# A fused attention and routed feed-forward kernel: a new order of VectorE's and GpSimd's step, and gelus, scores and k's remainder read from PSUM

## The reference, cut to what matters

```python
def _mlp(x, W1, b1, W2, b2):
    return gelu(x @ W1 + b1) @ W2 + b2              # [.., 256] -> [.., 256]

n = layernorm(x)
q, k, v = _mlp(n, ..q), _mlp(n, ..k), _mlp(n, ..v)
scores = tril(q @ k.T / sqrt(256 * 512))            # no softmax
out = layernorm(scores @ v) * ln_w + ln_b
x = x + out
tile = argmax(position_table @ sign(tile_sigs).T)   # one of 8 tiles for each position
x = x + layernorm(x) @ W[tile].T + b[tile]
```

## Time and profile before

| | before |
|---|---|
| median of 3 runs | 330.68 us (329.66 to 331.28) |
| the profiled execution | 329.83 us, of it 328.1 us span |
| mean granted TensorE clock | 0.947 of full |
| TensorE matmul busy | 281.4 us, 86% |
| TensorE weight load busy | 252.1 us, 77% |
| VectorE busy | 232.0 us, 71% |
| ScalarE busy | 202.5 us, 62% |
| GpSimd busy | 196.8 us, 60% |

### The profile page before, as it was taken

How to read it: one execution, slowest core, us unless ns; L and a number is a source line. 1 busy time by engine, 2 the same in 40 slices (tenths; PEclk the granted TensorE clock), 3 DMA queues, 4 the chain that set the end, 5 groups by cost and what they waited for, 6 DMA issues and landing times.

```text
span 328.1 us, 5585 instructions
## 1 busy us (share of the span) xinstructions
PE 281.4 (86%) x1828; PEld 252.1 (77%) x1828; DVE 232.0 (71%) x538; ACT 202.5 (62%) x402; POOL 196.8 (60%) x227
## 2 busy tenths in 40 slices
PE   5899999799989998899899999999998969996000
PEld 5778988698779888787878898899887969996000
DVE  3799759778987768865876787679569798885000
ACT  2377576667566884587468856966774469991000
POOL 3533506451664787589638854964793557777772
PEclk9579999999999999999999999999999999999555
DMA  8806940200020012001201040100047414943210
GB/s 213 284 0 212 337 156 1 67 31 0 2 91 8 32 65 98 32 33 34 97 2 47 20 128 16 51 1 2 32 122 193 125 53 137 306 145 112 75 54 2
DMA packets 24656, 28.01 MB, mean 85 GB/s; under 512 B 4722, under 2 KB 22386, under 8 KB 24564
## 3 DMA queue, kind: packets, MB, share of 16 engines
q1 hardware_dynamic: 15764, 13.07, 13.6%
q0 software_dynamic: 3488, 8.99, 7.8%
q10 hardware_dynamic: 5376, 5.59, 5.4%
HBM read 13.99 MB, written 14.56 MB: 87 GB/s over the span
## 4 chain that ended last, share of the span: by engine, by line
PE 63%; DVE 17%; POOL 5%; issue 5%; ACT 5%; DMA 3%; POOLq 0%; SPq 0%; DVEq 0%; ACTq 0%
PE ring L427 35%; PE o_ps L427 9%; PE s_ps L427 6%; POOL out_dram L1477 5%; PE sc_ps L427 4%; DMA w_stage<-w1k 3%; PE w_ps L427 2%; DVE xres L1004 2%; PE ring L440 2%; PE ring L669 2%; PE ring L518 1%; DVE hT L930 1%; DVE state L976 1%; DVE kT L942 1%; DVE v L955 1%
## 5 line engine op out<-in xcount | busy, mean ns | idle before, releaser
L427 PE MATMUL ring<-xnT,w_sp 128*128 128x512 f32 x288 | 75.1, 408 | 3.1 <-DVE xnT L925 1.7
L427 PEld LDWEIGHTS ring<-xnT,w_sp 128*128 128x128 f32 x288 | 54.0, 195 | 15.6 <-issue 2.0
L427 PE MATMUL ring<-hT,w_sp 128*128 128x512 f32 x192 | 47.4, 398 | 4.5 <-DVE qT L936 3.0
L726 ACT ACTIVATE h<-ring,b_cols 128x512 f32<-128x512 f32 x48 | 33.0, 687 | 21.1 <-PE ring L427 20.7
L427 PEld LDWEIGHTS ring<-hT,w_sp 128*128 128x128 f32 x192 | 35.0, 188 | 14.2 <-DVE qT L936 4.1
L1392 POOL DMA_INDIRECT sorted_rows<-xres,slot_i x32 | 33.8, 1057 | 8.6 <-issue 6.1
L1356 POOL TENSOR_TENSOR hT<-h,hT 128x512 fp32r<-128x512 f32 x24 | 31.7, 1331 | 4.5 <-ACT hT L729 4.3
L1362 POOL TENSOR_TENSOR vtok<-v,vtok 128x512 fp32r<-128x512 f32 x14 | 17.7, 1284 | 23.8 <-ACT vtok L749 23.8
L1381 POOL TENSOR_TENSOR xres<-ve,half 128x4 f32<-128x4 f32 (+1 forms) x9 | 8.7, 968 | 37.2 <-DVE ve L1024 37.1
L729 ACT CAST hT<-h 128x512 fp32r<-128x512 f32 x48 | 29.8, 620 | 1.5
L976 DVE TENSOR_TENSOR state<-s_ps,state 128x512 fp32r<-128x512 f32 x27 | 18.6, 688 | 16.5 <-ACT state L768 16.5
(11 more groups left out here) (181 smaller groups left out, 635.8 us busy)
## 6 DMA issues: line engine op xcount, KB each, us to landing
sorted_rows<-blank ACTq DMA_DIRECT2D x1, 5070.0 KB, 20.3
xt<-x SPq DMA_DIRECT2D x8, 512.0 KB, 3.6
slot_rows<-sorted_rows SPq DMA_DIRECT2D x23, 130.0 KB, 4.0
h<-sorted_rows SPq DMA_DIRECT2D x16, 130.0 KB, 2.7
w_stage<-tile_w SPq DMA_DIRECT2D x8, 256.0 KB, 4.0
hT<-position_table POOLq DMA_DIRECT2D x1, 512.0 KB, 7.1
sorted_rows<-xres,slot_i POOLq DMA_INDIRECT x32, 2.7
row_stage<-rows ACTq DMA_DIRECT2D x1, 384.0 KB, 8.1
```

What stands on the lines that cost most here:

```text
L427: last = te.matmul(o, lhs[k][a], rhs[k][c], start=start and k == 0 and i == 0, stop=stop and k == n - 1 and i == 2, skip_group_check=check)
L726: nc.scalar.activation(h32[:, m, :], ring[(2 + m) % 3][:, :], ACT.Gelu, bias=b1c[:, m // 2, m % 2:m % 2 + 1]).then_inc(gelu, 1)
```

## The change

What it does, by engine:

- **ScalarE**: gelu of halves 0, 2, 4 writes back into its own `ring` bank, and the rounding copy reads it there. The lead norm's four chunks are spread: one after half 4, one after q, one between k and v, one between v's halves. The squares of chunks 2 and 3 follow half 5.
- **VectorE**: `h_rest` reads the `ring` bank, `k_rest` reads k's bank and adds the bias itself, the mask writes the scores back into `sc_ps`, and `scores_rest` reads them there (group 7 keeps `sc32`). `h_rest` of half 0 stands at the head of the step, that of 2 ahead of chunk 2's state, that of 4 ahead of chunk 3. `x1_stats` and `x1_var` of group s move from the end of step s to step s + 1, behind `h_rest` of half 0. Negation and epsilon of `lead_var` and `x1_var` go to GpSimd (two small operations each).
- **TensorE**: a bank whose half belongs to VectorE is free when `h_rest` is done, not when gelu is; v's second half and ktok wait for `k_lo` where they waited for `k_full`; the scores wait for `sc_lo` of the group before.
- **GpSimd**: the step is half 1, `residual(s + 1)`, half 3, `rstd_lead`, `rstd_x1`, two scatters, [step 3: `tile_shifted(4)`], half 5, `rstd_out`, two scatters, `v_rest`, `tile_shifted`. Group 0's four scatters move from step 2 to step 1, group 1's stay in step 2.

```diff
+            def bank_free(s, m):
+                if m in DVE_H:
+                    te.wait_ge(h_lo_dve, len(DVE_H) * s + DVE_H.index(m) + 1)
+                else:
+                    te.wait_ge(gelu, 6 * s + m + 1)
...
                     if m >= 3:
-                        te.wait_ge(gelu, 6 * s + m - 2)
+                        bank_free(s, m - 3)
...
                     if j < 3:
-                        te.wait_ge(gelu, 6 * s + 4 + j)
+                        bank_free(s, 3 + j)
...
-                        te.wait_ge(k_full, 2 * s + 1)
+                        te.wait_ge(k_lo, 2 * s + 1)
...
-                        te.wait_ge(k_full, 2 * s + 2)
+                        te.wait_ge(k_lo, 2 * s + 2)
...
             def hidden(s, m):
                 act.wait_ge(fill, FILLS * s + 3 + m)
-                nc.scalar.activation(h32[:, m, :], ring[(2 + m) % 3][:, :], ACT.Gelu,
+                full = ring[(2 + m) % 3][:, :] if m in DVE_H else h32[:, m, :]
+                nc.scalar.activation(full, ring[(2 + m) % 3][:, :], ACT.Gelu,
...
-                nc.vector.tensor_tensor(hT[:, m, 1, :], h32[:, m, :], hT[:, m, 0, :].bitcast(F32),
+                nc.vector.tensor_tensor(hT[:, m, 1, :], ring[(2 + m) % 3][:, :], hT[:, m, 0, :].bitcast(F32),
...
-                nc.vector.tensor_tensor(kT[:, 1, j, :], k32[:, j, :], kT[:, 0, j, :].bitcast(F32),
-                                        ALU.subtract).then_inc(k_lo, 1)
+                nc.vector.scalar_tensor_tensor(out=kT[:, 1, j, :], in0=ring[(10 + j) % 3][:, :],
+                                               scalar=b2c[:, K, j:j + 1], in1=kT[:, 0, j, :].bitcast(F32),
+                                               op0=ALU.add, op1=ALU.subtract).then_inc(k_lo, 1)
...
             def rstd_lead(s):
+                pool.wait_ge(aggr1, s + 1)
+                nc.gpsimd.tensor_scalar(nm1[:, :], mv1[:, :, 0], -1.0, None, ALU.mult)
+                nc.gpsimd.tensor_tensor(ve1[:, :], mv1[:, :, 1], eps[:, :], ALU.add).then_inc(var1, 1)
...
             for s in range(LAST):
...
+                h_rest(s + 1, 1)
+                residual(s + 1)
+                h_rest(s + 1, 3)
+                if s + 2 < STEPS:
+                    rstd_lead(s + 2)
+                if s:
+                    rstd_x1(s - 1)
+                if s > 1:
+                    rows_sorted(s - 1, (0, 1))
+                if s == 3:
+                    tile_shifted(4)
+                h_rest(s + 1, 5)
+                rstd_out(s)
```

More of the change, by code:

```diff
@@ L725, in hidden, with q_rounded @@
                 act.wait_ge(fill, FILLS * s + 3 + m)
-                nc.scalar.activation(h32[:, m, :], ring[(2 + m) % 3][:, :], ACT.Gelu,
+                full = ring[(2 + m) % 3][:, :] if m in DVE_H else h32[:, m, :]
+                nc.scalar.activation(full, ring[(2 + m) % 3][:, :], ACT.Gelu,
                                      bias=b1c[:, m // 2, m % 2:m % 2 + 1]).then_inc(gelu, 1)
                 act.wait_ge(gelu, 6 * s + m + 1)
[L729 to L736, removed]
+                nc.scalar.copy(hT[:, m, 0, :], full).then_inc(h_hi, 1)
+            def q_rounded(s, j):
+                if j == 0:
+                    act.wait_ge(o_ready, CH * s)
+                act.wait_ge(fill, FILLS * s + 9 + j)
+                nc.scalar.activation(qT[:, 0, j, :], ring[(8 + j) % 3][:, :], ACT.Identity,
+                                     bias=b2c[:, Q, j:j + 1]).then_inc(q_hi, 1)
             def k_rounded(s):
@@ L744, in k_rounded, with v_rounded @@
                     nc.scalar.copy(kT[:, 0, j, :], k32[:, j, :]).then_inc(k_hi, 1)
[L746 to L749, removed]
+            def v_rounded(s, j):
+                act.wait_ge(v_sum, 2 * s + 1 + j)
+                nc.scalar.copy(vtok[:, 0, 2 * j:2 * j + 2, :], v32[:, 2 * j:2 * j + 2, :]).then_inc(v_hi, 1)
             def scores_rounded(s):
@@ L1018, in x1_var @@
                 alone(dve, gate_dve)
+                if s:
+                    dve.wait_ge(shift3, s)
                 for c in cs:
@@ L1021, in x1_var @@
                 last.then_inc(aggr3, 1)
[L1022 to L1024 removed]
+                if s == LAST:
+                    dve.wait_ge(aggr3, part)
+                    nc.vector.tensor_scalar(nm3[:, these], mv3[:, these, 0], -1.0, None, ALU.mult)
+                    nc.vector.tensor_scalar(ve3[:, these], mv3[:, these, 1], EPS, None, ALU.add).then_inc(var3, 1)
             def tile_rest(t):
@@ L1227, in _ @@
             for s in range(LAST):
+                h_rest(s + 1, 0)
+                if s:
+                    x1_stats(s - 1, range(CH))
+                    x1_var(s - 1, range(CH))
                 state_rest(s, 1)
@@ L1236, in _ @@
                     lead_var(s + 2)
-                h_rest(s + 1, 0)
+                h_rest(s + 1, 2)
                 state_rest(s, 2)
@@ L1251, in _ @@
                     route_tables()
-                h_rest(s + 1, 2)
+                h_rest(s + 1, 4)
                 out_centred(s, 3)
-                h_rest(s + 1, 4)
                 if s == 3:
@@ L1273, in _ @@
                     scores_rest(s + 1)
+                    x1_final(s, (3,))
                     state_rest(s + 1, 0)
                     out_centred(s + 1, 0)
-                    x1_final(s, (3,))
-                    x1_stats(s, range(CH))
-                    x1_var(s, range(CH))
                 else:
```

90 lines of the change are left out of this document (36 added, 54 removed).

## The result

The changed kernel takes 335.99 us (median of 4 runs, 334.82 to 336.45) where the kernel before takes 330.17 beside it (4 runs): a ratio of 1.0167 [1.0126, 1.0209]. Forecast were 335.7 us, from 331.9 to 339.0.

What follows compares the result with a forecast made beforehand. TensorE was taken to bound the loop, GpSimd's output scatters the end. Terms 1.2 - 1.3 - 0.1 - 1.8 - 0.2 + 4.3 + 2.9 = +5.0 on 329.83 gave 334.8, or 335.7 us on the medians' scale; range 331.9 to 339.0.

Steps and rivals of the forecast that it cites:

- Step 3, the largest term: TensorE stands 6.5 us at tile 4's weights until GpSimd's tile_shifted(4) sets the tile at 154.2: net +4.3 us.
- Other waits -2.2: In step 3 VectorE and GpSimd catch up while TensorE stands, so smaller waits vanish: -2.2 us.
- The clock: TensorE's standing at tile 4 brings the 1.2 GHz level for 5.9 us: +2.9 us, bounds nothing and +5.0.
- Step 2: Residual moves to where VectorE reads PSUM; ktok's wait of 1.34 us goes: -1.8 us with small waits.
- Steps 0 and 1: q's remainder is ready sooner in both, against new bank waits in the second: -1.3 and -0.1 us.
- Front 0: Ahead of the loop's steps, TensorE's half 5 waits for h_rest(2), which stands behind the routing's argmax: +1.2 us.
- Steps 4 and 5: Bound by TensorE's own work: -0.2 us together.
- Step 6: v's second half waits about 1.0 us for k_lo, covered by the first normed slot's 1.49 us wait: 0.
- Gains don't come: Rival: steps 0 and 2 keep their lengths, as q's second half and ktok wait anyway: 338 us, chance 0.13.
- The clock holds: Rival: the stall at tile 4 without the clock's fall, or a shorter stall: 333 us, chance 0.20.
- Faster: Rival: GpSimd reaches tile_shifted(4) before TensorE, no stall or clock fall: 327 us, chance 0.07 including not as written.

Runs made afterwards that it cites:

- tile4_first: The changed kernel with tile_shifted(4) at the head of GpSimd's step 3, nothing else altered: 327.17 us, ratio 0.9903.
- keep_busy: The changed kernel with 26 matmuls, whose results nobody reads, ahead of TensorE's wait for tile 4 in step 3: 333.73 us, ratio 1.0085.
- tile4_res_all_late: tile4_res_late with GpSimd's residual behind rstd_out in all steps: 337.31 us on another chip, ratio 0.9876.
- res_late_h_sbuf: tile4_res_late with VectorE's three halves read from SBUF again and each bank free at gelu: 320.78 us, ratio 0.9708.
- tile4_res_late: tile4_first with GpSimd's residual of steps 0 and 1 back behind rstd_out: 320.55 us, ratio 0.971.
- tile4_res_late_2: tile4_res_late run once more, unaltered: 320.33 us, ratio 0.9692.
- tile4_h_sbuf: tile4_first with VectorE's halves read from SBUF again and each bank free at gelu: 325.78 us, ratio 0.9842.
- before_res_early: The kernel before with only GpSimd's half 1 and residual moved first in steps 0 and 1: 345.23 us on another chip, ratio 1.0066.

## Why the prediction was right, and where it was not

The time came within 0.3 us of 335.7. The stall and its clock were right; that the total came so close was luck: errors of 2.6 and 1.8 us in steps 0 and 1 met -1.5 in step 3, -1.0 in front 0 and -0.7 in step 6. In the profile 1.1 us of error is left (the span grew by 6.1 where the sum had 5.0), in the medians 0.8 (335.99 beside 330.17): with a fourth run the kernel before has a median 0.5 us below the 330.68 that the forecast built on.

- **Step 3, the largest term: right.** Forecast were tile 4 set at 154.2 and a standing of 6.5 us; measured 154.8 and 6.16. The chain from GpSimd's half 3 on took 9.7 us (145.16 to 154.83) for the 10.0 of the sum. That the two times agree so well is luck in part, since the step began 1.3 us later than in the kernel before. "Other waits -2.2" was -2.8 (tile4_first's 29.38 us against 32.14).
- **The clock: right in kind, 2.9 forecast, 2.2 measured** (keep_busy). The half speed was to hold for 5.9 us of work as after the kernel's start; it held from 152.9 to 159.7, of which TensorE worked 4.9 us. The standing read as 3.2 us is nearer 2.9: a mean of 0.69 between 303 and 304 puts the fall at 303.4.
- **Step 2: -1.8, as forecast.** Here `residual` did move to where VectorE reads PSUM. tile4_res_all_late shows that this is 0.5 us of it, and 2.6 over steps 2 to 5; a further 0.9 goes when VectorE's halves are read from SBUF again (res_late_h_sbuf); that the rest is VectorE's order is not shown.
- **Steps 0 and 1: the step that failed.** I forecast "-1.3" and "-0.1" and got +1.3 and +1.7. The prediction had the mechanism in hand: it said that an operation with both inputs in SBUF lasts as long as GpSimd's residual beside it, and then credited step 2 with the residual's move without asking what stands beside it in steps 0 and 1. There it meets the routing's scan and product, costed at their old 0.41 and 1.95 us. Without that collision the steps are 28.8 and 30.1 us (tile4_res_late), -2.4 and -1.7: I had under-counted the gain too. The forecast left the end of the routing in step 0 at 56.2, though two of its operations had been held there beside GpSimd's half 3:

```profile
52.15 1.03 DVE L1085 TENSOR_TENSOR rows_in<-sizes 128x32 f32<-128x32 f32 x1
53.21 1.25 DVE L1086 TENSOR_TENSOR_SCAN ends<-keep_all,rows_in 128x32 f32<-128x32 f32 x1
```

  In the new order half 3 comes earlier, and in tile4_res_late they take 0.18 and 0.24 us; `h_rest(4)` is done at 54.9, not 56.8, and q's second half doesn't wait at all.
- **The clock in steps 0 and 1** was no term at all: the forecast waits of 1.0 to 1.2 us were given none. It fell for 3.4 us in both, and in step 0 that cost 1.5 us (keep_busy), more than half of the step's error of 2.6.
- **Front 0: +1.2 forecast, +0.2 measured.** The bank waits came, as 1.69 us at half 3 and 0.36 at half 5. But the first product began at 12.76, not at 14.08 as in the profile before, where VectorE's remainder of the weights (L1149) had been held by GpSimd's residual of group 0 for 2.16 us; here it came ahead of it and took 0.69. And the clock rose sooner in this run:

```profile
16.00:17.00 1.00, 1.00 (x5) 0.81 (x4) 1.00 (x2) 0.97 (x2) 0.00 (x0) 0.81 0.42 148
```

  where the kernel before worked at 0.50 until 20. What decides when it rises isn't settled, nor what the bank waits cost. Of two pairs of profiles in which the clock rose at about the same time, one says 1.4 us (37.7 in tile4_res_late_2, 36.3 in res_late_h_sbuf), the other nothing (37.9 in tile4_first, 38.0 in tile4_h_sbuf, where TensorE waited 0.79 us for the counts and 1.26 for q's remainder instead).
- **Steps 4 and 5: right. Step 6: 0 forecast, -0.7 measured.** v's wait for `k_lo` was put at 1.0 us and came as 0.17, and the first slot waited 0.46 us where it had waited 1.49. The scatters keep their pace of 1.29 us, as forecast.
- **The rivals.** "Gains don't come" (0.13) named ktok and q's second half as the places; the gains stayed away elsewhere, by another mechanism. "The clock holds" (0.20) is out. "Faster" was out as long as tile 4 stood where it did; with both costs mended the change gives 10 us, more than the 7.5 us that I called all that could be won inside the loop: steps 0 and 2 come out at 28.8 and 29.0 us, shorter than the 29.3 that I had read off step 5 as TensorE's own, and 0.7 us is won in step 6.

## What to carry to other kernels

When an operation moves to another time on its engine, look up what the engine that shares SBUF with it does at that time in *every* pass of the loop, the odd first passes above all; a gain in one pass says nothing of the others. When work is put ahead of an item that only one pass has, count the chain up to it: one item put behind 10 us of other work cost more here than all the rest gained (8.5 us of stall and clock). And a wait of 2 us on TensorE costs more than 2 us when it takes the clock with it: 3.5 us in step 0 here.

## What the runs showed of the hardware

- **VectorE is held for nearly the whole of GpSimd's operation.** Scan 0.41 to 2.28 us and product 1.95 to 3.83 (3.42 in before_res_early) beside a residual of 2.4; two small products 0.29 to 1.22 and 1.24 beside halves of 1.29. GpSimd can be held too (1.29 to 2.16 in the changed kernel, a power of 1.04 to 2.80 in before_res_early, each begun beside VectorE's product). `h_rest` with one input in PSUM took 656 to 693 ns in all 24 cases; from SBUF in tile4_h_sbuf it took up to 1821 ns, 798 in the mean. The Trainium skill (GPSIMD Engine Reference, 1. Specifications) says that GpSimd shares its SBUF interfaces with VectorE, and that VectorE's operations with two SBUF inputs or in a mode of two ports contend with it; the rows agree for two inputs, and add that the held operation waits for the other's end: the product of step 1 began at 79.30, the residual ended at 81.31, and 1.8 us later the product was done.
- **Not every GpSimd operation holds it.** Beside GpSimd's power on 128x4 (88.68 to 89.72 in the changed kernel, 1.04 us) VectorE did two operations with two SBUF inputs (L1137, L1139) in 0.26 us each, the time that they took in the kernel before with GpSimd idle; tile4_res_late has the same beside the same power.
- **Single-input operations on SBUF can be held too:** L1097, with one input of 128x32, took 1.18 us instead of 0.18 beside GpSimd's half 3. Whether that is the mode of two ports no run tells.
- **Granted clock after a short standing.** In steps 0 to 2 it fell after 1.98 (tile4_h_sbuf), 1.99, 2.00, 2.30, 2.66 and twice 2.68 us, each time when TensorE was already back at work. It did not after 2.01 us in keep_busy, nor after 1.30 to 1.52 us in tile4_h_sbuf and the kernel before; after 1.34 it fell once (before_res_early) and once not the earlier trace rows. So the length of one standing alone doesn't tell. The low levels behind these lasted 3.2 to 3.4 us; behind the 1.34 and behind the two stalls of 6.2 us they lasted 6.8.
- **ScalarE is a little faster into and out of PSUM**, where the prediction had no row: gelu 662 ns into PSUM against 688 into SBUF, the rounding copy 588 from PSUM against 620 from SBUF (24 each, changed kernel). The Trainium skill (ScalarE: Activation LUTs, Step-by-step: what each stage is for) says that a result goes to PSUM faster than to SBUF; gelu's rows agree, with 26 ns.
